# Expert tiles: turning the normalised rows and the gated z without TensorE

## What is computed

```python
x = x + attention(layernorm(x), ctx, ctx)
h = layernorm(x)                                   # (8*512 rows, 2048)
q = h @ Wq.T                                       # (rows, 16)
scores = q @ keys.T                                # (rows, 64 experts)
top_vals, top_idx = top_k(scores, 16)
gate = scatter(softmax(top_vals), top_idx)         # (rows, 64)
z = h @ A.T                                        # (rows, 64 experts * rank 8 = 512)
z_gated = z * gate repeated 8 times
x = x + 2.0 * (z_gated @ B.T)                      # (rows, 2048)
```

## Time and profile before

| what | us |
|---|---|
| median of 3 runs (lowest, highest) | 2157.5 (2156.28, 2159.11) |
| the profiled execution, its own time | 2156.57 |
| its span, first to last instruction | 2154.8 |
| TensorE matmul busy | 2115.7 (98%) |
| VectorE busy | 1673.8 (78%) |
| ScalarE busy | 1337.5 (62%) |
| GpSimd busy | 1561.3 (72%) |
| mean granted TensorE clock | 1.000 of full speed |
| chain that ended last, TensorE's share | 82% |

### The profile page before, as it was taken

One profiled execution on the slowest core, in us unless ns is written; L12 is line 12 of the kernel. 1 busy time (PEld: TensorE's weight loads), 2 busy tenths in 40 slices (PEclk: granted clock), 3 DMA queues, 4 the chain that ended last, 5 costly groups with the idle time before them and its releaser, 6 DMA issues.

```text
span 2154.8 us, 29239 instructions
## 1 busy us (share of the span) xinstructions
PE 2115.7 (98%) x8920; PEld 1328.0 (62%) x8920; DVE 1673.8 (78%) x4051; ACT 1337.5 (62%) x3051; POOL 1561.3 (72%) x965
## 2 busy tenths in 40 slices
PE   5999999999999999999999999999999999999999
PEld 2455455455455455454454454888888888888887
DVE  7999999999999999999999999644444444444443
ACT  4786786786786786786765646644444455445441
POOL 6999999999999999999999988633343433333420
PEclk9999999999999999999999999999999999999999
DMA  7232333333333332333221246544545444444431
GB/s 282 97 108 103 120 111 103 120 111 103 121 109 103 121 109 103 122 109 103 103 89 64 83 168 239 171 158 166 175 164 174 159 166 165 158 166 172 164 119 59
DMA packets 110705, 287.50 MB, mean 133 GB/s; under 512 B 7168, under 2 KB 7296, under 8 KB 109568
## 3 DMA queue, kind: packets, MB, share of 16 engines
q1 hardware_dynamic: 110592, 286.19, 38.3%
HBM read 219.06 MB, written 67.11 MB: 133 GB/s over the span
## 4 chain that ended last, share of the span: by engine, by line
PE 82%; DVE 7%; POOL 6%; ACT 2%; issue 2%; DMA 1%; SPq 0%; DVEq 0%; ACTq 0%; POOLq 0%
PE pair L755 11%; PE pair L749 8%; PE out L581 6%; PE out L582 6%; PE out L583 6%; PE z L583 5%; PE z L582 5%; PE z L581 5%; PE pair L644 5%; PE evac L631 4%; PE evac L655 4%; PE evac L656 4%; PE lag L698 4%; PE pair L745 4%; PE tp L600 2%; POOL r_f L1804 2%
## 5 line engine op out<-in xcount | busy, mean ns | idle before, releaser
L1838 POOL TENSOR_TENSOR rows<-rows,cin 128x1024 f32<-128x1024 f32 x48 | 117.0, 2437 | 325.7 <-DMA rows<-out_dram 273.6
L755 PE MATMUL pair<-r_f,back 128*128 128x512 f32 x768 | 342.7, 597 | 0.5 <-DVE prod L1035 0.5
L1804 POOL TENSOR_TENSOR r_f<-prod 128x1024 f32<-128x1024 f32 x128 | 303.0, 2378 | 9.3 <-DVE prod L1033 7.4
L755 PEld LDWEIGHTS pair<-r_f,back 128*128 128x128 f32 x768 | 143.0, 190 | 192.7 <-issue 146.5
L749 PE MATMUL pair<-w_sb,wts 128*128 128x512 f32 x512 | 225.1, 592 | 1.4 <-ACT w_sb L1625 0.9
L1480 ACT ACTIVATE xn<-tp 128x512 f32<-128x512 f32 x94 | 55.1, 586 | 231.0 <-PE tp L600 230.9
L581 PE MATMUL z<-a_hi,xt 128*128 128x512 f32 x496 | 195.9, 395 | 0.0
L581 PE MATMUL out<-b_hi,zt_hi 128*128 128x512 f32 x492 | 194.3, 395 | 0.0
L583 PE MATMUL z<-a_hi,xt 128*128 128x512 f32 x496 | 193.4, 390 | 0.0
L582 PE MATMUL z<-a_lo,xt 128*128 128x512 f32 x496 | 193.3, 390 | 0.0
L582 PE MATMUL out<-b_lo,zt_hi 128*128 128x512 f32 x492 | 191.6, 389 | 0.0
(11 more groups left out here) (234 smaller groups left out, 5576.8 us busy)
## 6 DMA issues: line engine op xcount, KB each, us to landing
out_dram<-att_sb SPq DMA_DIRECT2D x32, 1024.0 KB, 4.2
rows<-out_dram SPq DMA_DIRECT2D x64, 512.0 KB, 3.8
cin<-out_dram SPq DMA_DIRECT2D x63, 512.0 KB, 4.0
xin<-in_x_dram SPq DMA_DIRECT2D x63, 512.0 KB, 4.1
vf<-in_ctx_dram SPq DMA_DIRECT2D x31, 1024.0 KB, 5.1
out_dram<-rows SPq DMA_DIRECT2D x62, 512.0 KB, 2.8
xf<-in_x_dram SPq DMA_DIRECT2D x30, 1024.0 KB, 5.3
stat_in<-in_x_dram SPq DMA_DIRECT2D x27, 1024.0 KB, 5.1
```

What stands on the lines that cost most here:

```text
L755: return nc.tensor.matmul(pair_ps[:, bank, :], back[:, 3 * bank + n, :], r_f[:, row, :], start=n == 0, stop=n == 2)
L1804: nc.gpsimd.tensor_tensor(dst, prod[:, slot, 0:2, :], prod[:, slot, 2:4, :], ALU.add).then_inc(add_done, 1)
L1838: nc.gpsimd.tensor_tensor(half, first, other, op).then_inc(c_added, 1)
```

## The change

From tile 4 on (`FIRST_SPREAD`) the rows no longer go through TensorE's transposes. A 128x128 turn is a turn inside each 32x32 block and an exchange of blocks between the four groups of 32 partitions. ScalarE now does the exchange while it normalises: in place of one 128x2048 operation a tile takes 16 operations, each from one group of 32 partitions to another (`norm_blocks`). VectorE then turns all 32x32 blocks in place (`turn_spread`, four operations of 128x512). The gated z of these tiles goes out to a DRAM scratch in four transfers that put its column blocks on other rows (`store_z`), comes back in one (`load_z`), and VectorE turns its blocks into the bank `zt`. The weights are laid out in the matching feature order on the host. On the way some steps are put in another order: the queries of tile u+1 are made ahead of the last output bank of step u, 12 of the 16 normalising operations stand at the end of ScalarE's step and the other 4 behind `zt_high` of the next, and on VectorE the statistics and the gating change places with other work.

```diff
@@ sizes and rules
+        FIRST_SPREAD = 4
+        SPREAD = P // 4
+        SPREAD_PARTS = 16
+        def spread(t):
+            return not (isinstance(t, int) and t < FIRST_SPREAD)
+        def spread_z(n):
+            return not (isinstance(n, int) and (n < FIRST_SPREAD or n >= TT))
+        def ahead(u):
+            return later_tile(u) and spread(u + 2)
@@ SyncE
+            def store_z(n):
+                sp.wait_ge(zg_ready, n)
+                rows_of = zg[:].rearrange("p (b f) -> p b f", b=4)
+                for c in range(4):
+                    sp.dma_start(z_rows.rearrange("(b j) (c f) -> c j b f", b=4, c=4)[c],
+                                 rows_of[SPREAD * c:SPREAD * (c + 1)]).then_inc(z_stored, 16)
+            def load_z(n):
+                sp.wait_ge(z_stored, 64 * (n - FIRST_SPREAD + 1))
+                sp.dma_start(zg[:], z_rows).then_inc(z_loaded, 16)
...
+                if a and spread_z(u + 1):
+                    store_z(u + 1)
                 if is_step(u, TT):
                     store_last(r)
                 elif b:
                     store_half(u, r, 0)
                     if later_tile(u + 1):
                         sp.wait_ge(out_stored, 16 * (2 * u - 1))
                         load_rows(k, 4 + r, 0)
+                    if spread_z(u + 1):
+                        load_z(u + 1)
                     store_half(u, r, 1)
@@ TensorE
-                    for q in range(4):
-                        queries(u, q)
+                    if is_step(u, 2):
+                        for q in range(4):
+                            queries(u, q)
...
-                if b and not (is_step(u, 1) or is_step(u, TT)):
+                if b and not (is_step(u, 1) or is_step(u, TT) or spread_z(u)):
                     turn_z()
...
-                if f and not is_step(u, 0):
+                if f and not (is_step(u, 0) or spread(u + 1)):
                     for q in range(4):
                         turn_tile(u + 1, q)
...
                     for q in range(4):
+                        if q == 3 and f and not is_step(u, 1):
+                            for part in range(4):
+                                queries(u + 1, part)
                         out_bank(q)
@@ VectorE
-                nc.vector.tensor_tensor(xt[:, 1, part, :], tp_ps[bank_of(t, q)][:], xt[:, 0, part, :].bitcast(F32),
+                turned_x = xt_full[:, q, :, :] if spread(t) else tp_ps[bank_of(t, q)][:]
+                nc.vector.tensor_tensor(xt[:, 1, part, :], turned_x, xt[:, 0, part, :].bitcast(F32),
                                         ALU.subtract).then_inc(tp_lo, 1)
+            def turn_spread(t, q):
+                if q == 0:
+                    dve.wait_ge(xn_part, SPREAD_PARTS * (t - FIRST_SPREAD + 1))
+                part = xn[:, q * 512:(q + 1) * 512]
+                nc.vector.transpose(part, part).then_inc(tp_full, 1)
...
+                if spread_z(u):
+                    dve.wait_ge(z_loaded, 16 * (u - FIRST_SPREAD + 1))
+                    dve.wait_ge(zt_lo_done, u - 1)
...
+                    nc.vector.transpose(zt_ps[:].rearrange("p m (c j) -> p m c j", c=4),
+                                        zg[:].rearrange("p (c m i) -> p m c i", c=4, m=KN)).then_inc(zt_ready, 1)
                 if not is_step(u, TT):
                     zt_low()
+                if later_tile(u):
+                    half_statistics(u + 2, (r + 3) % RING, 0)
+                if f and spread(u + 1):
+                    for q in range(4):
+                        turn_spread(u + 1, q)
@@ ScalarE
             def tile_high(t, q):
                 n = tp_at(t, q)
-                act.wait_ge(tp_ready, n + 1)
-                nc.scalar.activation(xt_full[:, q, :, :], tp_ps[bank_of(t, q)][:], ACT.Copy).then_inc(tp_full, 1)
+                if not spread(t):
+                    act.wait_ge(tp_ready, n + 1)
+                    nc.scalar.activation(xt_full[:, q, :, :], tp_ps[bank_of(t, q)][:], ACT.Copy).then_inc(tp_full, 1)
                 act.wait_ge(tp_full, n + 1)
                 nc.scalar.activation(xt[:, 0, 4 * q:4 * q + 4, :], xt_full[:, q, :, :], ACT.Copy).then_inc(tp_hi, 1)
+            def norm_blocks(t, slot, blocks):
+                if blocks[0] == 0:
+                    act.wait_ge(norm2_ready, 2 * t + 2)
+                    act.wait_ge(tp_lo, tp_at(t - 1, 3) + 1)
+                by_block = xn[:].rearrange("p (k c i) -> p k c i", k=KD, c=4)
+                for c in blocks:
+                    own = slice(SPREAD * c, SPREAD * (c + 1))
+                    for b in range(4):
+                        nc.scalar.activation(by_block[SPREAD * b:SPREAD * (b + 1), :, c, :],
+                                             rows[slot][own, b * 512:(b + 1) * 512].rearrange("p (k i) -> p k i", k=KD),
+                                             ACT.Identity, bias=shift2[own], scale=rstd2[own]).then_inc(xn_part, 1)
...
-                    if f:
-                        norm_tile(u + 1, (r + 2) % RING)
+                    if is_step(u, 2):
+                        norm_tile(3, 3)
                     zt_high()
+                    if f and spread(u + 1):
+                        norm_blocks(u + 1, (r + 2) % RING, (3,))
...
                 if later_tile(u):
                     tile_root(u + 2)
+                    if ahead(u):
+                        tile_scale(u + 2)
+                if f and not is_step(u, 1):
+                    copy_queries(u + 1)
+                if ahead(u):
+                    norm_blocks(u + 2, (r + 3) % RING, (0, 1, 2))
```

More of the change, by code:

```diff
@@ L897, in tile_step @@
                 if b:
-                    if not f:
+                    if not f or spread(u + 1):
                         pe.wait_ge(zt_hi_done, u)
@@ L1379, in tile_step @@
                     tile_mean(u + 2)
+                if a:
+                    gate_z()
+                add_out(1)
+                if f:
+                    tile_low(u + 1, 2)
+                    tile_low(u + 1, 3)
                 if is_step(u, TT - 1):
                     zt_low(TT)
+                if later_tile(u):
+                    invert_root(u + 2)
                 add_out(2)
                 add_out(3)
-                if later_tile(u):
-                    invert_root(u + 2)
             each_tile(dve, tile_step)
```

50 lines of the change are left out of this document (27 added, 23 removed).

## The result

The changed kernel takes 2211.97 us (2211.66 to 2212.3, four executions) where the kernel before took 2158.23 beside it: a ratio of 1.025, 95% interval 1.0233 to 1.0268. The prediction was 2151 us with a range from 2128 to 2184, so the result is above it.

A forecast was written before the change was run, and what follows sets the result against it. It took TensorE to bound the kernel at 25.32 us a step, then the row buffers' chain at 25.25: -2.0 over 25 steps, with the ends -6.1 from 2156.57, 2150.5; median 0.9 above, so 2151 us, range 2128 to 2184.

The forecast's parts named there:

- What TensorE sheds: Transposes leaving TensorE for tiles 4 to 31: 1.67 us for rows plus 0.42 for z, 2.09 us a step.
- The pieces at 0.707: ScalarE's 16 normalising operations a tile, 0.707 us from start to start, priced from the same operation on 128 partitions.
- The chain of the rows: Closed loop from VectorE's reciprocal through scale, 16 pieces, turns, route, tile_low, statistics and gating: 24.5 us a step.
- the pieces do not overlap: Rival: ScalarE's pieces wait at group changes, 0.80 to 0.83 us each; 25.9 to 26.3 us a step, 2170 to 2180; chance 0.27.
- The turns at 0.60: VectorE's four block turns of the rows at 0.60 us each, 2.40 a tile, bounds half of it and 1.2 us.
- The hold of `tile_low(0)`: VectorE's tile_low(0), now with two SBUF inputs, waits for GpSimd's fourth add and ends 0.50 us behind it.
- The chain of the row buffers: Loop from gating through z issues, store, loads, GpSimd adds, tile_low, statistics to gating: 25.25 us, setting the step.
- The return of z: z's four stores, one load and turn stay hidden: 7.4 us from the gating's end, wanted some 13 us behind it.
- The steps at the ends: First step without row turns gains 2.1 us; the next, still filling, and the last give about 2.0 together.
- The range: Whole-kernel time from 2128 to 2184 us, leaving out TensorE as the bound, slow turns, and slow turns with non-overlapping pieces.
- the forecast's own range: Kernel time if the forecast case holds, 2145 to 2162 us around 2151; that case had chance 0.45.

The follow-up runs named there:

- e4: The kernel before with z's path alone: gated z of tiles 4 to 31 through the DRAM scratch, rows left to TensorE; 2145.54 us, 0.995 of before.
- e1: The changed kernel with the gated z of all tiles turned by TensorE again, nothing through the DRAM scratch; 2183.06 us, 1.0171 of before.
- e10: The changed kernel with z turned by TensorE and ScalarE's pieces reordered, the loop over the groups written outermost; 2181.78 us, 1.0114 of before.
- e12: The changed kernel with z stores issued by ScalarE and turned rows going through PSUM, all work kept; 2187.54 us, 1.014 of before.
- e3: The changed kernel with VectorE's row turns written to PSUM banks and copied back by ScalarE, so tile_low reads PSUM and SBUF; 2185.76 us, 1.0133.
- e6: The changed kernel with z turned by TensorE and each piece written to the partition group it reads, exchange left out; 2152.8 us, 0.9978 of before.
- e9: The changed kernel with z stores issued by ScalarE, turned rows through PSUM and pieces in their own groups, exchange left out; 2146.1 us, 0.9945.
- e7: The changed kernel with turned rows through PSUM and pieces in their own partition groups, exchange left out; 2175.23 us, 1.0079 of before.
- e8: The changed kernel with z stores issued by ScalarE and pieces in their own partition groups, exchange left out; 2177.9 us, 1.0093 of before.
- e2: The changed kernel with each of ScalarE's 16 pieces written to the partition group it reads, exchange left out; 2195.62 us, 1.0174 of before.
- e5: The changed kernel with the four z stores issued by ScalarE ahead of the rows' scale instead of by SyncE; 2193.14 us, 1.0164 of before.
- e11: The changed kernel with z's load issued behind the second store of the rows; 2208.07 us, 1.0234 of before.

## Why the prediction was wrong

**What TensorE sheds** was right as far as a run shows it: 0.42 us for z's transposes, 0.38 measured in e4, where TensorE is the bound.

**The pieces at 0.707** was a step that failed. They are 0.84 apart, since each starts in another partition group. The chain of the rows is 26.2 us, not 24.5 (e1, e10, e12), and that alone takes away the gain: the rival "the pieces do not overlap" had 25.9 to 26.3 us a step and 2170 to 2180; e1 gives 2183. It had a chance of 0.27, and the forecast took 0.707 as the price of the same shape. That row is on 128 partitions, in which no group ever changes, so it was no evidence on this point.

**The turns at 0.60** were right: four in 2.49 us, (2.49 - 0.67) / 3 = 0.61, no matter that they turn in place.

**The hold of `tile_low(0)`** was right in place, cause and size: 0.55 us behind the fourth add, against 0.50. `tile_low(0)` took 2.10 us for an operation of 0.68. The page "SBUF — State Buffer" of the Trainium skill, section "SBUF: two separate sides", states that rule for VectorE with two SBUF inputs against a GpSimd operation that reads SBUF, and the trace agrees. Taking the hold away is worth 26 us from the changed kernel (e3).

**The chain of the row buffers** was the right chain, and the step that failed in the number: it was to be 25.25 us and is 27.7 in the step shown. Three terms were too small. From the first z issue to the store's issue it is 2.1 us instead of 1.55, above my upper bound of 1.79 (four issues 0.47 apart are 1.88 already): 1.8 us for the four and 0.3 until the store's issue. First load to first add took 5.01 instead of 4.08, partner load to third add 5.45 instead of 4.48. That is 0.54 + 0.93 + 0.97 = 2.44, and 25.25 + 2.44 = 27.69; the other links differ by 0.15 at most and cancel. I had priced the z transfers by their issues and allowed 0 to 0.4 us for what they do to others, while the change puts another 0.5 MB of z a tile onto the same DMA engines. Whether they make the loads longer can be asked of the late 20 steps of each trace, as means:

| kernel | z's transfers | first load to first add | partner load to third add |
|---|---|---|---|
| before | no | 3.98 | 4.67 |
| e1 | no | 4.26 | 4.78 |
| e6 | no | 4.12 | 5.13 |
| e4 | yes | 4.53 | 5.05 |
| after | yes | 4.97 | 5.16 |
| e9 | yes | 4.98 | 5.10 |

For the first load they do: 4.0 to 4.3 us without z, 4.5 to 5.0 with it, and of the 1.0 us between before and after about 0.7 go with z (after against e1). On the page, too, the row loads have 3.8 to 4.1 us without z's path and 4.3 to 4.6 with it. For the partner load it is not shown, since e6 has 5.13 without any transfer of z; where its 0.5 us come from stays open. The return of z stayed hidden, as predicted, though it took 10.3 us from the end of the gating to its turn at 1715.98, not 7.4: ScalarE takes the turned z at 1719.09, without a wait.

**The steps at the ends** were taken as a gain of 4.1 in all. The first step without row turns (from tile 2 to tile 3) does not run at TensorE's floor: it is 26.2 us where before has 25.3. The step ahead of it reads 26.5 instead of 24.1, but that is the marker, which now stands behind the second statistics; the output matmuls around it keep their pace. The last two are 24.35 and 21.1 instead of 25.3 and 23.65, so that the four come to about nothing. In the middle 26 steps of 27.4 instead of 25.3 make +55, and +54 is measured.

**The range** was too narrow for a reason of its own: each case let one chain be long. Pieces without overlap and longer loads lie on two chains that pass through the same VectorE queue, and e7, e8 and e9 show that what shortens one link need not shorten the step: taking the hold away gives 0.6 us a step over e2, moving the z issues 0.5, both 1.8. The traces show why. In e2, with quicker pieces, `tile_low(0)` comes up already under the third add in 15 of the late 20 steps; the second `tile_low` is then the one that the fourth add holds:

```profile
1720.04 2.40 POOL L1923 TENSOR_TENSOR rows<-rows,cin 128x1024 f32<-128x1024 f32 x1 [3.59 <-DMA cin<-out_dram]
1722.52 2.73 POOL L1934 TENSOR_TENSOR rows<-xin,rows 128x1024 f32<-128x1024 f32 x1
```

```profile
1721.58 1.41 DVE L1034 TENSOR_TENSOR xt<-xn,xt 128x512 fp32r<-128x512 f32 x1
1722.91 0.68 DVE L1374 SCALAR_TENSOR_TENSOR rows<-out,rows 128x512 f32<-128x512 f32 x1
1723.51 2.29 DVE L1034 TENSOR_TENSOR xt<-xn,xt 128x512 fp32r<-128x512 f32 x1
```

So most of the hold's price was gone in e2 before e7 removed it: from the end of the fourth add to the end of the gating the late steps take 4.1 us in e2 and 3.4 in e7. In e8 the store goes out earlier and the adds with it, `tile_low(0)` is caught by the fourth add in 19 of the 20, and the same stretch takes 4.9 us, so that of 1.1 us gained at the issues 0.8 go to the hold. Only e9, without the hold, keeps them. The early six steps are longer in every kernel with the rows' path, and the link that is longer there is the store of the half: 3.1 to 4.2 us until the load behind it as a mean, 2.7 to 2.9 in the late steps. Why that store takes longer stays open.

The top of the forecast's own range was also added too low: 0.24 us for the issues and 0.4 for the transfers are 16 us over 25 steps, so 2167 and not 2162.

The best kernel of the study with all work in it is e4, the z path alone, 0.995 of before (0.9933 to 0.9967).

## What to carry to other kernels

When work leaves the engine that is the bound, write down each closed chain with the new transfers in it, and price the old transfers in that stretch as slower too, not only the new ones. A row measured on 128 partitions does not price the same operation on changing groups of 32. Ask of a hold or a wait which operation it will catch once the chains have moved: shortening one link can bring another operation under it, and then the gain is given back. When a change has two halves, try each alone: here one half was worth 11 us and the other lost 27, and together they lost 54.

## What the runs showed that I had not expected

- ScalarE starts a 32x512 piece 0.70 us behind the last one in the same partition group, and 0.83 to 0.84 when either the group read or the group written is another.
- Four 64 KB issues take 1.80 us in a row, and an issue behind them stands 2.1 us behind the first; the earlier trace rows had 0.47 apart, which gives 1.88.
- In every step in which GpSimd's fourth add holds `tile_low(0)`, the operation ends 0.55 us behind the add, whatever it lost by the wait: its length goes from 0.7 to 2.8 us (after, e2, e5, e6, e8, e11).
- TensorE's granted clock was 1.00 (2.4 GHz) before and in e9 at 95% busy, and 0.98 and 0.93 in the two stretches shown of the changed kernel at 91%. Part of that time is at the lower level, 1.2 GHz: in the 3 us below, behind a wait of TensorE of 3.05 us that ended at 1701.91, the clock is 0.56. Over the run the output matmuls average 416 to 435 ns against 389 to 395 before; those of z keep 389 to 391.

```profile
1703.00:1706.00 3.00, 3.00 (x9) 1.98 (x7) 2.72 (x13) 0.20 (x1) 0.00 (x0) 0.56 0.26 104
```
